# Hybrid attention, expert and recurrence kernel: the middle stage's front in tiles, and the last combine shared between PE and DVE

## What is computed

```python
x = x + attention(layernorm(x))
x = x + ffn(layernorm(x))
x = x + recurrence(layernorm(x))     # h[t] = a[t] * h[t-1] + u[t], a and u from two gates
x = x + ffn(layernorm(x))

def ffn(x):                          # per block of 2048 tokens
    scores = softmax(x @ gate_weight.T)                 # 64 experts, in 8 groups
    topk_w, topk_i = top 6 of the experts in the 3 best groups
    slot = expert * 96 + min(arrival number, 95)        # capacity 96 rows per expert
    buf[slot] = x[token]                                # a later token overwrites slot 95
    out = (silu(buf @ Wg) * (buf @ Wu)) @ Wd            # per expert, 96 x 256 rows
    y = sum over the 6 choices of out[slot] * topk_w
    return y + (silu(x @ Sg.T) * (x @ Su.T)) @ Sd.T     # shared expert
```

## Time and profile before

| | us |
|---|---|
| median of 3 runs | 1287.74 (1283.13 to 1291.53) |
| the profiled execution | 1283.71 |
| its span | 1281.9 |
| PE busy | 985.2 (77%) |
| DVE busy | 523.4 (41%) |
| ACT busy | 728.9 (57%) |
| POOL busy | 423.7 (33%) |
| mean granted TensorE clock, share of full | 0.881 |

### The profile page before, as it was taken

The page is one execution under the profiler, slowest core; times in us unless marked ns, Lnnn a source line. Parts: engine busy times, 40 slices in busy tenths (PEclk is TensorE's granted clock), DMA queues, the critical chain, the costliest instruction groups (busy, mean ns, idle before and its releaser), DMA issues.

```text
span 1281.9 us, 18696 instructions
## 1 busy us (share of the span) xinstructions
PE 985.2 (77%) x6520; PEld 594.9 (46%) x6520; DVE 523.4 (41%) x1532; ACT 728.9 (57%) x960; POOL 423.7 (33%) x408
## 2 busy tenths in 40 slices
PE   4886868778887788787554999955587863999973
PEld 3633323322332323222334999943344442999962
DVE  7744431156221233230441333337776741333327
ACT  2285989999999999999101444414434400344420
POOL 3100000000222003234043565530098985556550
PEclk9878888998999998999686999976698976999985
DMA  9990000000111001100583999748133434899947
GB/s 352 394 393 31 1 1 1 1 17 1 42 47 37 17 16 60 39 20 6 148 254 92 292 295 289 177 118 273 50 116 117 123 109 106 243 293 284 261 72 305
DMA packets 94927, 176.11 MB, mean 137 GB/s; under 512 B 13119, under 2 KB 46880, under 8 KB 94833
## 3 DMA queue, kind: packets, MB, share of 16 engines
q1 hardware_dynamic: 58416, 130.55, 30.4%
q0 software_dynamic: 23616, 28.44, 10.4%
q10 hardware_dynamic: 12800, 15.93, 4.5%
HBM read 107.30 MB, written 83.72 MB: 149 GB/s over the span
## 4 chain that ended last, share of the span: by engine, by line
PE 32%; DVE 5%; DMA 3%; issue 3%; SPq 2%; POOL 2%; ACT 2%; DVEq 1%; POOLq 0%; ACTq 0%
PE PS L1323 13%; PE PS L1334 8%; PE PS L1261 4%; PE PS L1393 2%; PE PS L1310 2%; POOL expert_in L307 2%; SPq L1116 1%; DMA spare_space<-expert_out 1%; DMA normed<-xp 1%; SPq L1117 1%; PE PS L1246 1%; DMA XE<-expert_in 1%; PE PS L1270 1%; DMA expert_out<-ob,yidx 1%; POOL expert_out L1209 1%
## 5 line engine op out<-in xcount | busy, mean ns | idle before, releaser
L307 POOL DMA_INDIRECT expert_in<-xp,didx x192 | 192.9, 1005 | 621.7 <-ACT PR L684 483.9
L679 ACT ACTIVATE PR<-PS 128x1024 f32<-128x1024 f32 (+3 forms) x320 | 275.4, 935 | 55.7 <-PE PS L578 40.7
L684 ACT ACTIVATE PR<-PR 128x2048 f32<-128x2048 f32 (+3 forms) x160 | 272.4, 1705 | 0.0
L1209 POOL DMA_INDIRECT expert_out<-ob,yidx x128 | 180.6, 1411 | 148.2 <-ACT ob L1502 108.3
L587 PE MATMUL PS<-PR,V 128*32 128x512 f32 (+3 forms) x1280 | 164.8, 590 | 80.4 <-ACT PR L684 80.3
L575 PE MATMUL PS<-QT,KT 96*128 96x512 bf16 (+3 forms) x640 | 177.5, 372 | 19.8 <-ACT PR L679 16.9
L1740 DVE SCALAR_TENSOR_TENSOR gta<-gth,PS 88x192 f32<-88x192 f32 x128 | 44.8, 350 | 193.6 <-ACT gth L1492 193.6
L575 PEld LDWEIGHTS PS<-QT,KT 96*128 96x128 bf16 x640 | 59.3, 103 | 130.3 <-ACT PR L679 89.7
L1492 ACT ACTIVATE gth<-PS 88x192 f32<-88x192 f32 x128 | 41.7, 326 | 107.8 <-PE PS L1323 107.8
L1323 PEld LDWEIGHTS PS<-XT,spare_space 128*88 128x88 f32 x960 | 92.5, 164 | 8.8 <-issue 2.6
L1502 ACT ACTIVATE ob<-PS,wslot 96x256 f32<-96x256 f32 x128 | 60.1, 469 | 61.9 <-PE PS L1334 59.6
(11 more groups left out here) (257 smaller groups left out, 1355.3 us busy)
## 6 DMA issues: line engine op xcount, KB each, us to landing
spare_space<-in_wgu SPq DMA_DIRECT2D x60, 352.0 KB
expert_out<-zero SPq DMA_DIRECT2D x2, 8256.0 KB, 50.4
expert_in<-zero SPq DMA_DIRECT2D x2, 7776.0 KB, 39.3
XE<-expert_in ACTq DMA_DIRECT2D x32, 486.0 KB, 9.8
WGU<-in_wgu SPq DMA_DIRECT2D x44, 352.0 KB
spare_space<-expert_out SPq DMA_DIRECT2D x24, 512.0 KB, 6.1
spare_space<-in_wd SPq DMA_DIRECT2D x60, 176.0 KB
shared_space<-in_wgu SPq DMA_DIRECT2D x24, 352.0 KB
```

The costliest lines, as they stand in the source:

```text
L307: pool.indirect_dma_start(out=buf_d[f], out_offset=bass.IndirectOffsetOnAxis(ap=didx[b][:, r, j:j + 1], axis=0), in_=xp[b][:, r, :], in_of ...
L679: act.activation(PR[:, n % 3, 2 * pr:2 * pr + 2, cols(c, s):CW], PS[:, S0 + 2 * pr:S0 + 2 * pr + 2, cols(c, s):CW], ACT.Tanh, scale=1.0 / ...
L684: act.activation(PR[:, n % 3, :, lo:CW], PR[:, n % 3, :, lo:CW], ACT.Exp, scale=SOFT_CAP).then_inc(exp_done, 1)
L1209: pool.indirect_dma_start(out=y_d[f], out_offset=bass.IndirectOffsetOnAxis(ap=yidx[:, n % 4, j:j + 1], axis=0), in_=ob[:, i % EU, :], in_o ...
```

## The change

Five things are changed.

1. `turn_rows`, `turned_rows`, `logits` and, for the recurrence, `turn_recur` and `turned_recur` work tile by tile: the producer signals each tile (`row_tile`, `recur_tile`), two transposes follow, and ACT copies 256 columns instead of 1024. The tiles alternate between two PSUM banks; the third and fourth tile of a chunk wait until the first and second have been copied. This holds for k = 3 to 7 and for the four recurrence chunks.
2. The first chunk of results of the middle stage is added tile by tile inside `statistics(0, None)` by `add_first_tile`; the overflow product is added after the first tile; `results_free` rises at the last tile.
3. At c = 1, `statistics(2, 0)` is split into `statistics(None, 0)` and, behind it, `statistics(2, None)`; `slots` and `destinations` of k = 4 stand before `recur_inputs(1)`; `add_results(3)` stands behind `add_overflow(3)`, ahead of `recur_states(1)`.
4. PE's `place` stands ahead of `overflow_rows` (only c = 1 has both).
5. The last combine goes in five groups of tiles: 0 to 3, 8 to 11, 4 to 7, 12 and 13, 14 and 15. The third and the last are summed on PE (overflow product plus four products with the identity matrix into the same PSUM place), the others on DVE. Chunk 3 has a buffer of its own, so its loads wait for nothing. There are five stores.

```diff
             def turn_rows(k):
-                pe.wait_ge(rows_ready, k + 1)
...
-                for h in range(CH):
-                    for r in range(CT):
-                        last = pe.transpose(PS[:, T0 + h, r * P:(r + 1) * P], xp[k % NXP][:, r, h * P:(h + 1) * P], const("ident"))
-                last.then_inc(rowsT_psum, 1)
+                for r in range(CT):
+                    if r < CT - 1:
+                        pe.wait_ge(row_tile, (CT - 1) * n + r + 1)
+                    else:
+                        pe.wait_ge(rows_ready, k + 1)
+                    if r >= 2:
+                        pe.wait_ge(rowsT_ready, CT * n + r - 1)
+                    for h in range(CH):
+                        at = (r // 2) * C + h * P
+                        last = pe.transpose(PS[:, T0 + r % 2, at:at + P], xp[k % NXP][:, r, h * P:(h + 1) * P], const("ident"))
+                    last.then_inc(rowsT_psum, 1)
...
             def turned_rows(k):
-                act.wait_ge(rowsT_psum, n + 1)
-                act.activation(xnT[:], PS[:, T0:T0 + 2, :], ACT.Copy).then_inc(rowsT_ready, 1)
+                for r in range(CT):
+                    act.wait_ge(rowsT_psum, CT * n + r + 1)
+                    act.activation(xnT[:, :, r * P:(r + 1) * P],
+                                   PS[:, T0 + r % 2, (r // 2) * C:(r // 2 + 1) * C].rearrange("p (h n) -> p h n", h=CH), ACT.Copy)\
+                       .then_inc(rowsT_ready, 1)
...
+            def combine_late():
+                pe.wait_ge(xt_ready, NH * 2)
+                pe.wait_ge(o95_loaded, 32)
+                pe.wait_ge(out_copied, 2 * E)
+                for n in LATE_DVE:
+                    dropped_late(*LATE_ORDER[n], True).then_inc(late_psum, 1)
+                for n in LATE_PE:
+                    lo, hi = LATE_ORDER[n]
+                    for i in range(lo, hi):
+                        c, r = i // CT, i % CT
+                        dropped_late(i, i + 1, False)
+                        pe.wait_ge(late_ld[c][r], 16)
+                        for j in range(NACC):
+                            last = pe.matmul(late_bank(i), const("ident"), late_results[c][:, r, j * C:(j + 1) * C], start=False,
+                                             stop=(j == NACC - 1), skip_group_check=True)
+                    last.then_inc(rows_summed, 1)
...
             # PE, inside the loop over c
+                if c:
+                    place(k)
                 if c + 2 < NC:
                     overflow_rows(c + 2)
-                if c:
-                    place(k)
...
+            def add_first_tile(r):
+                if r == 1:
+                    dve.wait_ge(ov_psum, 1)
+                    xc = X[:, 0:CT, :].rearrange("p r n -> p (r n)")
+                    dve.tensor_tensor(xc, xc, PS[:, S0:S0 + 2, :].rearrange("p b n -> p (b n)"), ALU.add).then_inc(ov_added, 1)
+                dve.wait_ge(y_ld[r], 16)
+                tables = GB[:, r, :].rearrange("p (j n) -> p j n", j=NACC)
+                dve.tensor_tensor(tables[:, 0:2, :], tables[:, 0:2, :], tables[:, 2:4, :], ALU.add)
+                dve.drain()
+                dve.tensor_tensor(tables[:, 0, :], tables[:, 0, :], tables[:, 1, :], ALU.add)
+                dve.drain()
+                added = dve.tensor_tensor(X[:, r, :], X[:, r, :], tables[:, 0, :], ALU.add)
+                if r == CT - 1:
+                    added.then_inc(results_free, 1)
+                dve.drain()
...
             # DVE, inside the loop over c
-                if c:
+                if c == 1:
+                    statistics(None, 0)
+                    statistics(2, None)
+                elif c:
                     statistics(c + 1 if c + 1 < NC else None, c - 1)
...
-                if c == 1:
-                    add_results(3)
                 if c:
                     shift(k)
                     choose(k)
+                if c == 1:
+                    slots(k)
+                    destinations(k)
                 if c < NC:
                     recur_inputs(c)
                 if c + 2 < NC:
                     add_overflow(c + 2)
-                if c:
+                if c == 1:
+                    add_results(3)
+                if c >= 2:
                     slots(k)
                     destinations(k)
```

138 lines of the change are left out of this document (76 added, 62 removed).

## The result

The changed kernel takes 1281.59 us (median of 13 runs, 1276.55 to 1289.70) beside 1288.0 (median of 13, 1282.83 to 1292.36) for the kernel before: ratio 0.9953, 95% interval 0.9932 to 0.9973. That is 6.1 us, where 6.5 was forecast (and 1281.2 for the time). One slow execution in all that follows, of early_no_pacing_2 (1451.07 at a granted clock of 0.704), is left out of that kernel's ratio. The profiled execution of the changed kernel took 1279.33, with a span of 1277.5 and a mean granted clock of 0.891 (before: 1283.71, 1281.9, 0.881).

The account below looks back on a forecast made before the run. Bound: PE in the expert stages, POOL's scatters in the middle stage, DVE's adds and the loads close together in the tail. Gains 1.6 + 2.0 + 2.9 = 6.5 us from the median 1287.74 gave 1281.2, range 1275 to 1288.

Parts of the forecast that it names:

- (d): Middle stage, second chunk's step: placement and list 4 moved ahead, so chunk 4's first scatter comes 5.9 us earlier.
- (a): Chunk 3's front in tiles, before the first expert stage: gain 1.0 to 2.0 us, taken as 1.6.
- (b): First chunk of the middle stage, results added by tile: net gain 0.2 us, between a loss of 0.5 and a gain of 1.4.
- (c): Middle stage, chunk 4's statistics alone and logits in tiles: gates of chunk 1 end at 917.0 instead of 920.24.
- (e): Middle stage, chunk 3's results moved ahead of the recurrence's states: list 5 0.6 us late, bounds 1 early and 3 late.
- Slack of list 5: Middle stage: chunk 5's scatters could start 2.6 us sooner, so an earlier first scatter shortens the stage by at most that.
- The middle stage: Forecast gain between the expert stages: 2.6 - 0.6 = 2.0 us, with 0 and 5.9 as bounds.
- The rival in which the middle stage gives nothing: List 5 comes 2.6 us or more late, so the kernel takes 1283 to 1285 us; chance 0.15.
- (f): Tail, the last combine split between PE and DVE with five stores: gain 2.9 us, bounds 1.3 and 3.7.
- The rival in which PE stays at 1.2 GHz: Tail: PE's clock stays low and PE becomes the bound, 4.7 us worse there, kernel time 1288.8 us; chance 0.10.
- The marks: Profile signs, including chunk 4's first scatter about 7.5 us earlier, a POOL wait at chunk 5, last sums 5 us after loads.
- three signs of being wrong: No POOL wait at chunk 5; PE's second group ending after DVE's chunk 2; last load later than 1270 less 3.6.

Follow-up runs that it names:

- early_no_pacing_2: Changed kernel with chunk 3's results added ahead of chunk 4's routing and no memsets spacing the scatters of chunks 4 to 6, on chip 11: ratio 1.0204 to the kernel before.
- after_again: The changed kernel run again as it is, on another chip (chip 11): ratio 0.9968 to the kernel before.
- first_chunk_undone: Changed kernel with the first chunk's results added as before (whole adds, then statistics); executed once, no ratio; list 4 came 2.0 us earlier than in the changed kernel.
- order_undone: Changed kernel with the second chunk's step on DVE and PE back in its order of before: ratio 0.9957 to the kernel before.
- results3_early: Changed kernel with only the adding of chunk 3's results put back ahead of chunk 4's routing: ratio 0.9935 to the kernel before, median 1278.83 us.
- tail_only: Kernel before with only the new last combine, chunk 3's own buffer and the five stores: ratio 0.9974 to the kernel before, 3.3 us.
- no_pacing: Changed kernel without the memsets that space the scatters of chunks 4 to 6, on chip 5: ratio 0.9903 to the kernel before.

## Why the prediction was right, point by point

- **The sum.** 6.5 forecast, 6.1 measured by the ratio. From the stage's start, the profiled pair gives 3.2 up to the last scatter (454.42 to 451.22; forecast 3.6) and 2.8 behind it (2.9 forecast). The forecast held by parts, though within the first of them the terms were off both ways. The fit of the parts is luck in some measure: of the five profiles with this front and middle stage and spaced scatters four stand 3.1 to 3.6 ahead of the kernel before at the last scatter, but after_again only 0.3, and behind it the ten new tails take 1.9 to 4.6 less than the kernel before. One slip in the working: by its own numbers the gates of chunk 1 end at 917.2 and not 917.0, which makes the 5.9 of (d) a 5.7 and moves nothing else, since the slack caps it.
- **(a), front in tiles: 1.6 forecast, 2.3 in the pair.** Taken over all kernels with it, A is 26.2 to 26.6 seven times and 27.4 to 27.8 four times, against 28.75 to 29.03 in the three without. The two groups are the two cases of the step on the clock: in the kernel after the granted clock is 1.00 from 641.5 on, 3 us into the shared passes, in after_again only from 647.0, 6 us into them. The 16 shared passes in front of the placement took 8.07 in the kernel after, where they end as DVE's selection does (646.5), and in after_again

```profile
640.92 9.68 PE L1270 MATMUL PS<-xnT,sgu 128*96 128x512 f32 x16
```

  9.68, where half of the gain is lost. DVE's first tile to the logits is 2.60 instead of 4.52, the 1.9 of the forecast's 2.0. So the mechanism was right, and the taken value lay between two cases instead of on either. The copies of 256 columns took 0.38 each, for 0.4 assumed. One such copy agrees with what the Trainium skill's "ScalarE: Activation LUTs", section What ACT_TABLE_LOAD costs, gives for it (186 ns + 256 x 0.833 = 0.40). Its overlap of 93 ns back to back is seen where both tiles stand ready, as for chunk 4, where two copies take 0.63 together:

```profile
901.27 0.63 ACT L1485 ACTIVATE xnT<-PS 128x256 f32<-128x256 f32 x2
```

  The pair at 633.79 took 0.81, since each copy waited there for its own transposes.
- **(b), first chunk: 0.2 forecast.** The states of chunk 0 stand 34.26 behind the first add before and 33.58 after, 0.7 gained. What the forecast did not do is follow the later loads past these states: first_chunk_undone prices the new form at 2.0 on list 4, in one execution. That the front's gain is lost against DVE's queue was right (32.39 without the later loads). The step named the later loads and sized them well (DVE's add over chunk 1 is 1.2 late, for 1.65 forecast), and then dropped them.
- **(c), (d), list 4 earlier: 5.9 forecast** beyond the gain of (a). By B it is 6.9 (72.53 to 65.64); without (b) it would have been 8.9. Right in kind, low by 1.0. In the time it brought nothing, as order_undone shows; the forecast had capped it by the slack of list 5.
- **(e), list 5: 0.6 late forecast, 1.25 measured** (110.22 to 111.47). The states of chunk 1 were given as 929.8 and came at 927.38 (74.03 by B, 0.56 late). The price set for PE's gap was right in its own row (transposes 0.93 longer, for 0.9) and wrong in its effect: results3_early has neither gap nor slow transposes and takes as long to list 5. The step that failed is letting PE's clock carry the lateness; in its place stand the 0.6 of the states and 0.7 behind them of which the cause is open.
- **Slack of list 5: 2.6 forecast.** POOL reached chunk 5 4.83 early, as forecast in kind, and its first scatter there came 1.34 earlier by B. But only 0.43 is left at the last scatter, since the 24 scatters of chunk 5 then took 40.73 instead of 39.89: two of them last 1.99 and 1.87 at its head, before only one. List 5 to last scatter is 111.5 in each spaced kernel whose list 5 binds, and 113.3 before, so the true slack was 1.8. The middle stage, forecast at 2.0, gave 0.4: this is the term that was mis-sized most, by 0.8 in the slack and 0.7 in the lateness, and what (a) gave above its forecast, 0.7, with 0.5 of the first expert stage (202.18 to 201.67 from chunk 3's first scatter to the first add), covered most of it. That is luck: in after_again (a) gave 1.1 and the first expert stage was 0.8 longer than before. The rival in which the middle stage gives nothing had 0.15 and came nearer the truth in its place than the forecast did.
- **(f), the tail: 2.9 forecast, 2.85 in the pair** (36.23 to 33.38 from the load to the span's end), 3.3 by the ratio of tail_only. Of the pair's 2.85, 2.2 lie up to DVE's last add and 0.7 behind it, where the last store is half as large (0.6 forecast). The last add was to end 30.5 behind that load and ended 30.65. Inside, two misses cancel. PE's gap was to be 3 us with 2.4 lost to the clock; it was 1.41 and the next sums took 1.99 a tile as the ones before, so nothing was lost. And tile 14 was met 24.7 behind the dropped rows' load instead of 23.2, chunk 2's last tile 20.9 instead of 19.5. So PE ended 29.2 behind that load, for 29.7 forecast, and DVE, on later tiles, became the bound by 1.4. The rule weighed there, the Trainium skill's "TensorE: Matmul & The Clock Gate", section Why this matters for your kernels, on idle gaps between bursts, is not contradicted: the gap that it warns of did not come about. The rival in which PE stays at 1.2 GHz is refuted: chunk 1's sums ran at 1.99 for four matmuls from 1259.67 on, against 3.15 ahead of them.
- **The marks.** Three showed: a first scatter of chunk 4 9.7 earlier against the stage's start (7.5 forecast), a new wait at chunk 5, and PE's sums of the last two tiles done 4.5 behind the landing of the first (5 forecast). One of the three signs of being wrong came: the last load landed later than allowed, by the 1.5 just named (chunk 3's last tile 25.9 behind the dropped rows' load instead of 24.5). It cost nothing, as the clock's loss did not come.

## What to carry to other kernels

Moving work out of idle time to bring one thing forward is paid where it is put: chunk 3's adds left an idle stretch of DVE and made the next list 3.6 later, which used up the gain; ask of each piece moved what stands behind it in its new queue, and follow it to the next chunk, not only to the next mark. In a stage that a paced issuer sets, an earlier start is worth no more than the slack of the next list, and that slack is measured to the last item, not to the next head. A buffer whose loads start later because it is released only with its last tile can cost more (2.0 on list 4 here, in one execution) than the split adds save (0.3 forecast). And a guard such as the memsets between scatters is not to be dropped on the word of one chip: where no_pacing gained, the trouble that the memsets keep away did not show in any of four profiles.

## What the runs showed of the hardware that was not expected

- The rise of TensorE's clock within 16 shared passes comes at one of two places from execution to execution: 8.0 to 8.3 or 9.4 to 9.7 us for the same 16 in the eleven profiles with the new front, in the same kernel too (8.07 and 9.68).
- 5.55 us of idle PE doubled the next eight transposes (1.97 against 1.04), and 1.41 us changed nothing in the sums behind it (1.99 before and after).
- A scatter issued every 1.28 instead of 1.58 us, over 24 in a row, could bring ACT, DVE and PE to a standstill of 10 us, and DVE alone to one of 14 us at the one chunk behind the first expert stage that no kernel spaces; two groups of runs show it and one does not, with the same instructions.
- The first scatter of chunks 4 to 6 takes 1.83 to 2.02 us in nearly every profile, the ones behind it mostly 0.97 to 0.99. It isn't the wait on a list: chunk 3's first one takes 0.99 behind a wait of 26 us, and in the kernel before chunk 5's takes 1.87 with no wait.
